# The last gathers of a mixture-of-experts layer: wait for the last tile that is used, fetch the lower rows two at a time and add them one by one, the upper rows by threes

## The reference, cut to what matters

```
xf = layernorm(x).reshape(2048, 512)
scores = softmax(xf @ gate_w)
_, sel = top_k(scores + expert_bias, 2)           # two of 8 experts for each token
routed_in = xf[token_idx] * top_scores_sorted     # 4096 rows, sorted by expert
h = silu(ragged_dot(routed_in, w1, counts)) * ragged_dot(routed_in, w3, counts)
routed_out = ragged_dot(h, w2, counts)
out = silu(xf @ sw1) * (xf @ sw3) @ sw2           # the shared expert, for all tokens
out = out.at[token_idx].add(routed_out)
x = x + tanh(g_ffn[1]) * out
```

## Time and profile before

| | |
|---|---|
| median of 3 runs | 1345.48 us (1344.13 to 1347.64) |
| the profiled execution's own time | 1356.95 us |
| its span in the profile | 1355.3 us |
| TensorE matmul busy | 1260.3 us (93%) |
| VectorE, ScalarE, GpSimd busy | 654.7 (48%), 446.5 (33%), 409.6 us (30%) |
| mean granted TensorE clock | 0.971 of full |

### The profile page before, as it was taken

The page is one execution under the profiler, slowest core; times in us unless marked ns, Lnnn a source line. Parts: engine busy times, 40 slices in busy tenths (PEclk is TensorE's granted clock), DMA queues, the critical chain, the costliest instruction groups (busy, mean ns, idle before and its releaser), DMA issues.

```text
span 1355.3 us, 18346 instructions
## 1 busy us (share of the span) xinstructions
PE 1260.3 (93%) x6226; PEld 1064.6 (79%) x6227; DVE 654.7 (48%) x1104; ACT 446.5 (33%) x755; POOL 409.6 (30%) x333
## 2 busy tenths in 40 slices
PE   5999989999999999999999979997999999999970
PEld 4788868888888888888888868886788888888860
DVE  6555356544356656565465466765232232223216
ACT  3333342233243523443343347550222222222210
POOL 2221112000022211321244142257656240017844
PEclk8999999999999999999999989998999999999985
DMA  6821367554649855885966231155445242224447
GB/s 199 273 86 56 102 217 287 186 196 175 225 182 347 302 221 194 331 306 194 273 251 221 68 89 39 33 183 202 170 136 186 78 159 74 74 76 154 141 155 256
DMA packets 88395, 240.42 MB, mean 177 GB/s; under 512 B 8300, under 2 KB 35144, under 8 KB 76040
## 3 DMA queue, kind: packets, MB, share of 16 engines
q1 hardware_dynamic: 64824, 160.19, 32.9%
q0 software_dynamic: 23040, 79.08, 18.1%
q10 hardware_dynamic: 464, 0.27, 0.1%
HBM read 163.75 MB, written 75.76 MB: 177 GB/s over the span
## 4 chain that ended last, share of the span: by engine, by line
PE 86%; DVE 4%; DMA 3%; issue 3%; ACT 1%; another core or an unknown queue 1%; POOL 1%; ACTq 0%; SPq 0%; DVEq 0%
PE bank L1160 26%; PE bank L1330 19%; PE bank L1188 12%; PE bank L1368 10%; PE bank L1085 4%; PE bank L1105 4%; PE bank L1115 2%; PE bank L1297 2%; PE bank L1348 1%; PE bank L1132 1%; DMA fin_high<-y_all,slr 1%; PE bank L1071 1%; DVE wl L1507 1%; POOL fin_high L777 1%
## 5 line engine op out<-in xcount | busy, mean ns | idle before, releaser
L1160 PE MATMUL bank<-xTh,G 128*128 128x512 f32 x1024 | 278.6, 397 | 1.8 <-DVE xTl L1613 1.8
L1330 PE MATMUL bank<-W,dxh 128*128 (+2 forms) x880 | 207.6, 378 | 23.8 <-DVE dmid L1767 11.5
L1160 PEld LDWEIGHTS bank<-xTh,G 128*128 128x128 f32 x1024 | 188.8, 188 | 42.6 <-issue 3.4
L1330 PEld LDWEIGHTS bank<-W,dxh 128*128 128x128 f32 x880 | 164.6, 192 | 40.4 <-issue 25.1
L1188 PE MATMUL bank<-DN,bhh 128*128 128x512 f32 x512 | 157.9, 390 | 0.0
L1160 PE MATMUL bank<-xTl,G 128*128 128x512 f32 x512 | 137.3, 390 | 0.0
L1368 PE MATMUL bank<-W,dhh 112*128 (+1 forms) x440 | 126.6, 410 | 5.4 <-issue 5.1
L1635 DVE SCALAR_TENSOR_TENSOR bs<-bank,tab,bs 128x512 f32<-128x512 f32 x64 | 47.5, 742 | 160.9 <-PE bank L1160 160.9
L1767 DVE TENSOR_TENSOR dmid<-bank,dsg 128x448 f32<-128x448 f32 x55 | 34.2, 622 | 177.8 <-ACT dsg L970 173.4
L1188 PEld LDWEIGHTS bank<-DN,bhh 128*128 128x128 f32 x512 | 96.2, 188 | 21.3 <-issue 1.7
L1160 PEld LDWEIGHTS bank<-xTl,G 128*128 128x128 f32 x512 | 96.1, 188 | 20.7
(11 more groups left out here) (250 smaller groups left out, 1989.9 us busy)
## 6 DMA issues: line engine op xcount, KB each, us to landing
G<-gate_up_split SPq DMA_DIRECT2D x48, 1024.0 KB, 7.0
DN<-down_split SPq DMA_DIRECT2D x24, 1024.0 KB, 4.9
wst<-in_L_ffn_w POOLq DMA_DIRECT2D x24, 896.0 KB, 5.9
gate_up_split<-G SPq DMA_DIRECT2D x16, 1024.0 KB
y_all<-dys SPq DMA_DIRECT2D x55, 256.0 KB
xs_sorted<-zero POOLq DMA_DIRECT2D x3, 3328.0 KB, 20.8
xsd<-xs_sorted SPq DMA_DIRECT2D x39, 256.0 KB, 3.0
down_split<-DN SPq DMA_DIRECT2D x8, 1024.0 KB
```

The lines of the kernel that those rows point to most:

```text
L1160: mm = pe.matmul(bank[m][:, :], G[:, c % 2, f, h, m, i, :], a[b % 2][:, i, :], start=(n == 0), stop=(n == 3 * DC - 1))
L1330: mm = pe.matmul(bank[o][:, 0:width], a[par][:, k, :], w[:, bass.ds(slot, 1), at + k * step:at + k * step + width].rearrange("p a n -> p ( ...
```

## The change

It computes two more numbers and rewrites the end of GpSimd's and VectorE's programs.

- `need`: in `results()` VectorE takes the largest low address and the largest of all addresses of each partition (`most`); TensorE turns the two columns into rows of bank 6, VectorE takes their maxima, adds 128 and shifts right by 7. With these inputs that gives 45 and 52 tiles.
- Low gathers: GpSimd waits for the first 45 tiles, then issues seven gathers into buffers that are free by then (`row` 1 to 7, where the sorted rows were built), waits for `d_down` of tile 51 (`s_dd`, last + 16 = 52), and issues nine into `fin_low`. Each waits until the gather two before it has landed.
- High gathers: they wait for the stores of the first 52 tiles instead of 55; each waits until the gather three before it has landed; the ring has 12 buffers instead of 8.
- VectorE adds each low tile when it has landed, ahead of `d_hid(54)` instead of behind it, and then the high tiles as before.

```
@@ results()
-                chain(dve.tensor_tensor(slr[:, 0, :], slf[:, 0, :], slf[:, 1, :], ALU.min))
+                chain(dve.tensor_tensor(low_f[:, :], slf[:, 0, :], slf[:, 1, :], ALU.min))
+                dve.tensor_copy(slr[:, 0, :], low_f[:, :])
+                chain(dve.tensor_reduce(most[:, 0:1], low_f[:, :], AX.X, ALU.max))
+                chain(dve.tensor_reduce(most[:, 1:2], slf[:, :, :].rearrange("p a t -> p (a t)"), AX.X, ALU.max))
@@ TensorE, between d_down(14) and d_x(16)
             pe.wait_ge(s_slot1, 2)
+            for i in range(2):
+                mm = pe.transpose(bank[6][0:1, i * P:(i + 1) * P], most[:, i:i + 1], ident)
+            mm.then_inc(s_rank1, 1)
@@ VectorE, behind d_hid(15)
+            dve.wait_ge(s_rank1, 2)
+            chain(dve.tensor_reduce(need_f[0:1, :], bank[6][0:1, 0:2 * P].rearrange("p (a n) -> p a n", a=2), AX.X, ALU.max))
+            chain(dve.tensor_scalar(need_f[0:1, :], need_f[0:1, :], float(P), None, ALU.add))
+            chain(dve.tensor_copy(need_i[0:1, :], need_f[0:1, :]))
+            dve.tensor_scalar(need_i[0:1, :], need_i[0:1, :], 7, None, ALU.logical_shift_right).then_inc(s_slot1, 1)
@@ GpSimd, the end (SOON = 7, HIGH = 12)
+            def stored(count):
+                for i in range(2):
+                    pool.wait_ge(s_dst[i], (count + 1 - i) // 2 * 16)
+                    alone(None)
+            def low(t):
+                if t >= 2:
+                    pool.wait_ge(s_yg[(t - 2) % 4], 16 * (TT // 4 + (t - 2) // 4 + 1))
+                pool.indirect_dma_start(low_at[t], None, y1_dram,
+                                        bass.IndirectOffsetOnAxis(ap=slr[:, 0, t:t + 1], axis=0)).then_inc(s_yg[t % 4], 16)
+            pool.wait_ge(s_slot1, 3)
+            stored(pool.value_load(need_i[0:1, 0:1], min_val=TT + 1, max_val=TT + NT1))
+            for t in range(SOON):
+                low(t)
             last = pool.value_load(tend1_i[0:1, E1 - 2:E1 - 1], min_val=1, max_val=NT1 - 1)
-            half = (last + TT + 1) // 2
-            for i in range(2):
-                pool.wait_ge(s_dst[i], half * 16)
-                alone(None)
+            pool.wait_ge(s_dd, last + TT)
+            alone(None)
+            for t in range(SOON, TT):
+                low(t)
+            stored(pool.value_load(need_i[0:1, 1:2], min_val=TT + 1, max_val=TT + NT1))
             for t in range(TT):
-                pool.indirect_dma_start(fin_low[:, t, :], None, y1_dram,
-                                        bass.IndirectOffsetOnAxis(ap=slr[:, 0, t:t + 1], axis=0)).then_inc(s_yg[t % 4], 16)
-            for i in range(2):
-                pool.wait_ge(s_dst[i], 16 * ((TT + NT1 + 1 - i) // 2))
-            for t in range(TT):
-                if t >= 8:
-                    pool.wait_ge(s_x4, t - 7)
-                pool.indirect_dma_start(fin_high[:, t % 8, :], None, y1_dram,
-                                        bass.IndirectOffsetOnAxis(ap=slr[:, 1, t:t + 1], axis=0)).then_inc(s_rsc[t % 8], 16)
+                if t >= 3:
+                    pool.wait_ge(s_high[(t - 3) % HIGH], high_count(t - 3))
+                if t >= HIGH:
+                    pool.wait_ge(s_x4, t - HIGH + 1)
+                pool.indirect_dma_start(fin_high[:, t % HIGH, :], None, y1_dram,
+                                        bass.IndirectOffsetOnAxis(ap=slr[:, 1, t:t + 1], axis=0)).then_inc(s_high[t % HIGH], 16)
@@ VectorE, the end
+            dve.wait_ge(s_sha, TT)
+            for t in range(TT):
+                dve.wait_ge(s_yg[t % 4], 16 * (TT // 4 + t // 4 + 1))
+                last = dve.scalar_tensor_tensor(out=xres[:, t, :], in0=low_at[t], scalar=gates[:, 3:4],
+                                                in1=xres[:, t, :], op0=ALU.mult, op1=ALU.add)
             d_hid(TT + NT1 - 1)
-            dve.wait_ge(s_sha, TT)
-            for i in range(4):
-                dve.wait_ge(s_yg[i], 2 * 16 * TT // 4)
-            for t in range(TT):
-                last = dve.scalar_tensor_tensor(out=xres[:, t, :], in0=fin_low[:, t, :], scalar=gates[:, 3:4],
-                                                in1=xres[:, t, :], op0=ALU.mult, op1=ALU.add)
             chain(last)
```

More of the change, by code:

```diff
@@ L48 @@
 NT1 = 2 * TT + E1 - 1
+SOON = 7
+HIGH = 12
 G_W = HID + E1
@@ L115, in program @@
         bias8 = keep("bias8", [P, E1])
-        pace = keep("pace", [P, 32])
+        pace = keep("pace", [P, 48])
         wlim = keep("wlim", [P, DC])
@@ L203, in program @@
         dmid, dhh, dhl, dys = (dmid0, dmid1), (dhh0, dhh1), (dhl0, dhl1), (dys0, dys1)
-        wst1, wst2, row, sel1, mask1, upto1, before1, base1, nt1, tend1, tst1, tex1, tex1_i, tend1_i, slf, slw, slr, rsc = run(
+        wst1, wst2, row, sel1, mask1, upto1, before1, base1, nt1, tend1, tst1, tex1, tex1_i, tend1_i, slf, slw, slr, rsc, low_f, most, need_f, need_i = run(
             WKV, ("wst1", [P, 2048]), ("wst2", [P, 2048]), ("row", [P, 4, D]), ("sel1", [P, TT, E1]), ("mask1", [P, E1, TT]),
@@ L207, in program @@
             ("tex1_i", [P, 48], I32), ("tend1_i", [P, E1], I32), ("slf", [P, 2, TT]), ("slw", [P, 2, TT], I32),
-            ("slr", [P, 2, TT], I32), ("rsc", [P, 2, TT]))
+            ("slr", [P, 2, TT], I32), ("rsc", [P, 2, TT]), ("low_f", [P, TT]), ("most", [P, 2]), ("need_f", [P, 2]), ("need_i", [P, 2], I32))
         rows_at = [row[:, i, :] for i in range(4)] + [row4[:, :], row5[:, :]] + [place(f"row{6 + i}", [P, D], X_A + (20 + 2 * i) * KB)[:, :] for i in range(2)]
@@ L217, in program @@
         tcmp1 = place("tcmp1", [P, 48, E1 - 1], RING + 1024)
-        fin_low, fin_high = run(W_AT, ("fin_low", [P, TT, D]), ("fin_high", [P, 8, D]))
+        fin_low, fin_high = run(W_AT, ("fin_low", [P, TT - SOON, D]), ("fin_high", [P, HIGH, D]))
+        low_at = rows_at[1:8] + [fin_low[:, i, :] for i in range(TT - SOON)]
         ident = cst[:, C_ID:C_ID + P]
@@ L354, in program, with high_count @@
         tok_v = tok.rearrange("b (i p) -> (b i) p", p=P)
+        s_high = s_rsc + s_xg
+        def high_count(t):
+            i = t % HIGH
+            return 16 * ((2 * TT // 8 if i < 8 else len(range(i - 8, NT0, 4))) + t // HIGH + 1)
         x_rows = x.rearrange("b s d -> (b s) d")
@@ L1910, in _ @@
                                              op0=ALU.mult, op1=ALU.add).then_inc(s_sha, 1)
-            d_hid(TT + NT1 - 1)
-            dve.wait_ge(s_sha, TT)
-            for i in range(4):
-                dve.wait_ge(s_yg[i], 2 * 16 * TT // 4)
-            for t in range(TT):
-                last = dve.scalar_tensor_tensor(out=xres[:, t, :], in0=fin_low[:, t, :], scalar=gates[:, 3:4],
-                                                in1=xres[:, t, :], op0=ALU.mult, op1=ALU.add)
+            dve.wait_ge(s_sha, TT)
[3 more added lines that the diff above has]
+                                                in1=xres[:, t, :], op0=ALU.mult, op1=ALU.add)
+            d_hid(TT + NT1 - 1)
             chain(last)
             for t in range(TT):
-                dve.wait_ge(s_rsc[t % 8], 16 * (2 * TT // 8 + t // 8 + 1))
-                dve.scalar_tensor_tensor(out=xres[:, t, :], in0=fin_high[:, t % 8, :], scalar=gates[:, 3:4],
+                dve.wait_ge(s_high[t % HIGH], high_count(t))
+                dve.scalar_tensor_tensor(out=xres[:, t, :], in0=fin_high[:, t % HIGH, :], scalar=gates[:, 3:4],
                                          in1=xres[:, t, :], op0=ALU.mult, op1=ALU.add).then_inc(s_x4, 1)
```

## The result

| | before | change |
|---|---|---|
| median | 1346.2 us (1342.99 to 1347.95, 13 runs) | 1352.15 us (1348.23 to 1358.83, 13 runs) |
| ratio to before, 95% interval | | 1.0053 (1.0039 to 1.0067) |
| the profiled execution's own time | 1356.95 us | 1351.85 us |
| its span | 1355.3 us | 1350.2 us |

A forecast was written before the change was run, and what follows sets the result against it. TensorE bounds up to about 1300 us, then chains of waits in the last 55 us. Tail -5.5 and front +0.3 give -5.2, a span of 1350.1; with the 11.5 us between profile and median carried over, 1340.3; range 1335 to 1347.

The forecast's parts named there:

- Front of the change: Counting of needed tiles ahead of `d_x(16)`: TensorE charged 0.3 us, VectorE nothing, up to 0.8 us without cover.
- Start of the low gathers: GpSimd, free at 1287.8, issues the first low gather at 1288.9 instead of 1299.3, 10.4 us earlier.
- Pairs: Low gathers paced by landings: flight 3.4 us plus restart 0.26, so 3.66 us per pair against 2.5 unpaced.
- Rival (3): At the second low gather's landing: flights of 5.2 us make pairs take 5.46, time 1352.9, slower; chance 0.08.
- GpSimd blocked by the adds: Rival: some 25 gathers each wait for a VectorE add of 0.75, 19 us lost, about 1359; chance 0.05 with another.
- First high gather: Leaves at 1318.2, 6.8 us before 1324.99; that is 39.5 us after ScalarE's copy of tile 49 starts.
- The last tile behind the adds: Output stores queue behind tile 54, itself behind 16 low adds: first output store about 1325, or 1330, not 1334.1.
- High gathers with the cap: At most three in flight: six intervals of 1.36, nine of 1.6; last add at 1345.6 against 1351.10.
- rival (1): High gathers fly 6.18 us beside output stores, so three in flight leave 2.15 apart: 1346.6, no change; chance 0.17.
- The base: Profiled execution (1356.95) lies 11.5 us over the median of 1345.48; that difference was carried over to the forecast.
- Rival (2): ScalarE's late copies of tiles 53 and 54 belong to profiling; the change brings 3 us: 1342.5, no change; chance 0.08.

The follow-up runs named there:

- the front alone: The kernel before plus only the counting of needed tiles (reductions, two transposes, four small operations), counts unused: 1345.79 us, ratio 1.0016 (1.0000 to 1.0033).

## Why the prediction was wrong

The forecast was 1340.3 us and faster; it is slower, outside the range. By its steps:

- **Front of the change: mis-sized.** "VectorE nothing; without that cover it would cost up to 0.8 us." The cover from `dxh` was there (in the change's trace `dxh` ends at 960.43 and `dxl(16)` starts at 961.01, 0.58 late); what wasn't looked at is who works beside. GpSimd's weight operations of 4.04 us run at that very place, and a cast of two numbers ended with one in three traces of seven. The runs of the front alone give 2.2 us where I put 0.3, but the interval (0 to 4.4) doesn't exclude that. The step's error was to price the four by their size.
- **Start of the low gathers: right** but for 1.4 us, reading `need`.
- **Pairs: nearly right.** 3.66 forecast, 3.8 up to the seventh and 3.94 from there: the flight was 3.2 to 4.0, then 3.6 to 4.5 (3.4 forecast). Rival (3) did not come; that its 1352.9 lies beside the measured 1352.15 is chance.
- **"GpSimd blocked by the adds": the step that failed most.** I gave this rival and another 0.05 together, because 16 high gathers had taken 1016 ns in the median beside adds. Those rows were real, and the rule was real as well: `pace` stood 4.39 us, and seven low gathers took 1.34 instead of 0.95. The Trainium skill (SBUF — State Buffer, SBUF: two separate sides) names "two SBUF inputs (only against a GpSimd op that reads SBUF)" among what takes the shared port. The adds have two SBUF inputs, and `pace` reads SBUF. By that page the pair is held "for the whole instruction"; that it can be a whole row of seven instructions the page doesn't say. The runs show 4.39, 4.57, 4.66 and 4.75 us for `pace` and 4.80, 5.55, 5.64, 5.66 and, beside twelve adds, 7.36 us for a gather.
- **First high gather: 39.5 forecast, 46.2.** Of the 6.7 us, 1.4 are the start, 4.2 the held `pace`, the rest the pairs and what lies between. The early start was used up wholly.
- **The last tile behind the adds: right in kind, and nearly free.** Tile 54 is copied at 53.4, not 45.8, since the low gathers ended 6.9 us later than forecast. With it at 33.2 the tail was only 0.7 us shorter.
- **High gathers with the cap: between forecast and rival (1).** 22.6 us from first to last forecast, 25.7 measured: 1.35 up to the eighth (1.36 forecast), then (1341.86 - 1325.67) / 8 = 2.02, near the rival's 2.15; three flights were 6.9 to 7.4. Without the cap 1.33 all through. Rival (1) alone, priced at no change, was right on this term: the cap costs 4 us of tail.
- **The base.** "The profiled execution (1356.95) lies 11.5 us over the median of 1345.48; I carry the difference over". Profiling isn't what makes the difference: the front's kernel, profiled, took its median. That execution had a stop of its own ahead of the tail, and late copies in it. Rival (2) saw the late copies and put them down to profiling; they are missing in one profiled execution of three. The undisturbed tail, from that one trace, is 75.0, with the high gathers at 40.8. Against it the forecast's own first high gather would have won 1.3 us, not 6.8.

Against the forecast the tail is 8.8 us longer (80.2 for 71.4): 6.7 up to the first high gather, 3.1 under the cap, less 1.0 behind the last gather.

The account against the kernel before closes within the interval: tail 80.2 - 75.0 = 5.2 us, front some 2.2, together 7.4; the ratio of 1.0053 is 7.1 us of 1346.2 (5.2 to 9.0). With the tail of 76.6 in its place it would be 5.8, inside as well, so which of the two tails the plain runs of before have isn't shown.

## What to carry to other kernels

Before moving VectorE work next to GpSimd work, list what GpSimd issues in the same microseconds, and let the bad bound price even the smallest operation at the length of what runs beside it, a whole row of VectorE operations included. Leave gaps in a backlog that is worked off while GpSimd still has gathers to issue. And align two traces at a mark just ahead of the change before comparing spans: here a stop in one execution was larger than the change.

## What the hardware showed beyond that

- A gather of 256 KB flew 3.2 to 4.5 us while few others did, 4.3 to 7.4 beside 512 KB output stores. Issuing it takes 0.95 us, 1.34 beside a lone add.
- Beside a row of 28 unpaced gathers ScalarE stood for 30.7 us and TensorE for 27.6, and the copy of tile 54 came 10 us late in two of three traces with the tail of before (a row of 16); with two to four in flight it never did. What the engines waited for stays open: no run separated it.
- The small cast ends within 0.1 us of GpSimd's operation; the one-column addition within 0.1 us of VectorE's row (1298.45 against 1298.40); a gather that stood beside VectorE's row ends 0.81 to 0.83 us after it.
